# Moving LayerNorm scaling from VectorE to GpSimd and the value eviction to ScalarE in a fused attention and mixture-of-experts block

## The reference

```python
# x: (4, 512, 256), 16 heads of 16, 8 experts, top 1, all float32
h = layernorm(x) * (1 + ca) + sa                 # ca, sa, ... : rows of silu(c) @ wmod, one set per batch
qkv = h @ Wqkv.T + bqkv                          # bqkv: 768 values, the last 256 belong to v
attn = softmax(mask(q k^T / 4)); o = attn v      # causal
x = x + ga * (o @ Wout.T + bout)
h = layernorm(x) * (1 + cb) + sb
x = x + gb * (shared_mlp(h) + s * expert(h))     # expert = argmax of h @ router, s = sigmoid of its logit
```

## Time and profile before

| what | value |
|---|---|
| median of 3 runs | 481.53 us |
| the profiled execution's own time | 479.8 us |
| its span | 478.1 us |
| mean granted TensorE clock | 0.967 of full speed |
| TensorE (PE) busy | 402.4 us, 84% |
| VectorE (DVE) busy | 310.0 us, 65% |
| ScalarE (ACT) busy | 226.8 us, 47% |
| GpSimd (POOL) busy | 209.0 us, 44% |
| chain that ended last | PE 51%, DVE 17%, DMA 8%, POOL 7%, issue 7%, ACT 6% |

### The profile page before, as it was taken

How to read it: one execution, slowest core, us unless ns; L and a number is a source line. 1 busy time by engine, 2 the same in 40 slices (tenths; PEclk the granted TensorE clock), 3 DMA queues, 4 the chain that set the end, 5 groups by cost and what they waited for, 6 DMA issues and landing times.

```text
span 478.1 us, 8357 instructions
## 1 busy us (share of the span) xinstructions
PE 402.4 (84%) x2898; PEld 227.9 (48%) x2898; DVE 310.0 (65%) x629; ACT 226.8 (47%) x403; POOL 209.0 (44%) x251
## 2 busy tenths in 40 slices
PE   3767677889978789988879968999968999999991
PEld 3233233444544345444434434565645666666661
DVE  3823697876898968999977753789734444444441
ACT  2533424867666666755677636345122232323220
POOL 1457393374226763358331762110600555555332
PEclk9997789999999999998999989999989999999998
DMA  8568548765678557652433001994621344434210
GB/s 258 170 154 212 147 117 259 265 196 136 168 264 293 156 127 167 222 179 88 169 81 99 2 0 52 354 360 161 180 86 44 65 80 85 78 74 81 32 21 0
DMA packets 45921, 67.95 MB, mean 142 GB/s; under 512 B 5365, under 2 KB 33653, under 8 KB 45881
## 3 DMA queue, kind: packets, MB, share of 16 engines
q1 hardware_dynamic: 40200, 58.76, 40.6%
q0 software_dynamic: 5152, 8.14, 8.6%
q10 hardware_dynamic: 528, 0.52, 0.3%
HBM read 43.14 MB, written 25.18 MB: 143 GB/s over the span
## 4 chain that ended last, share of the span: by engine, by line
PE 51%; DVE 17%; DMA 8%; POOL 7%; issue 7%; ACT 6%; SPq 3%; ACTq 0%; DVEq 0%; POOLq 0%
PE bank L1411 35%; DVE mx L1066 5%; PE bank L1525 4%; PE bank L1509 3%; DVE rowg L1167 2%; PE bank L1739 2%; PE bank L1481 2%; DMA qk_d<-W 2%; POOL W L719 2%; DMA w_d<-rowg 2%; DMA mod_d<-h2T 1%; ACT rowg L896 1%; DMA stage<-in_gup 1%; POOL rowg L727 1%; POOL rowg L726 1%
## 5 line engine op out<-in xcount | busy, mean ns | idle before, releaser
L846 ACT ACTIVATE W<-bank 128x512 f32<-128x512 f32 (+1 forms) x176 | 94.8, 564 | 65.1 <-PE bank L1509 63.3
L1066 DVE TENSOR_REDUCE mx<-bank 128x1 f32<-128x384 f32 (+3 forms) x176 | 104.8, 632 | 20.2 <-PE bank L1483 19.9
L1411 PE MATMUL bank<-W 128*128 128x256 f16 (+2 forms) x756 | 106.5, 293 | 10.2 <-POOL W L694 3.4
L1411 PEld LDWEIGHTS bank<-W 128*128 128x128 f16 x756 | 73.3, 100 | 44.3 <-issue 14.2
L1481 PE MATMUL bank<-W 126*128 126x128 f16 (+3 forms) x256 | 67.0, 318 | 20.6 <-DVE mx L1066 17.2
L719 POOL TENSOR_SCALAR_AFFINE_SELECT W<-W 128x512 f32<-128x512 f32 x64 | 45.3, 713 | 79.7 <-ACT W L846 79.7
L1411 PE MATMUL bank<-W,h2T 128*128 x276 | 68.4, 385 | 4.9 <-DVE W L1182 4.0
L1509 PE MATMUL bank<-W 128*128 128x512 f16 (+3 forms) x256 | 63.1, 304 | 5.2 <-ACT W L846 3.5
L789 POOL DMA_INDIRECT out<-h2T,sidx x23 | 36.3, 1578 | 69.5 <-DVE h2T L1381 69.2
L1525 PE MATMUL bank<-W 128*32 128x128 f32 (+3 forms) x512 | 48.4, 451 | 8.7 <-POOL W L719 8.7
L1483 PE MATMUL bank<-maskb,identb 128*128 128x128 bf16 (+2 forms) x176 | 45.3, 257 | 0.0
(11 more groups left out here) (163 smaller groups left out, 522.7 us busy)
## 6 DMA issues: line engine op xcount, KB each, us to landing
w_d<-rowg SPq DMA_DIRECT2D x18, 512.0 KB, 3.9
W<-w_d SPq DMA_DIRECT2D x18, 512.0 KB, 8.0
stage<-in_gup SPq DMA_DIRECT2D x16, 512.0 KB
qk_d<-W SPq DMA_DIRECT2D x48, 128.0 KB
W<-qk_d SPq DMA_DIRECT2D x32, 192.0 KB, 4.4
stage<-in_down SPq DMA_DIRECT2D x8, 512.0 KB
x_sb<-in_x SPq DMA_DIRECT2D x4, 512.0 KB, 8.9
h_d<-gbb SPq DMA_DIRECT2D x4, 512.0 KB, 4.5
```

The source lines that it names most:

```text
L846: a.activation(PT[j][:, i:i + m, :], t_bank(N)[:, 0:m * w].rearrange("p (i n) -> p i n", i=m), ACT.Exp).then_inc(s_exp, 1)
L1066: v.tensor_reduce(mx_v[:, b % 2, hp0 // 4, par, i:i + m, t], SB[N % 3][:, 0:m * w].rearrange("p (i n) -> p i n", i=m), AX.X, ALU.max).then ...
L1411: i = t_.matmul(outp, l, r, start=(n == 0), stop=(n == len(prods) - 1), **kw)
```

## The change

Both normalisations are computed by GpSimd: `norm1` moves there as it is, and what `scale2` did becomes the first of three instructions of GpSimd's `modulate2`. The eviction of the values moves to ScalarE, one scaled copy of 128x512 in place of two VectorE instructions of 128x256, and no bias is added. The value bias is instead multiplied by the output weights once, by two float32 matmuls of TensorE in the lead (`value_bias`), and VectorE adds the row to the output bias. The broadcast load of the value bias is gone (`bvb`), and its semaphore count falls from 48 to 32. The signature, the new semaphores and the list of inputs change to suit and are left out here.

```diff
@@ -162,7 +162,7 @@
         cs = sb("cs", [P, 2, KC, B])
         sac = sb("sac", [P, KC, B])
         cac = sb("cac", [P, KC, B])
-        bqk = sb("bqk", [P, 4])
+        bqk = sb("bqk", [P, 6])
         st1 = sb("st1", [P, NT, 6])
         mv1 = sb("mv1", [P, NT, 2])
         ve1 = sb("ve1", [P, NT])
@@ -221,7 +221,7 @@
         h1 = early(2 * KC * S, F16).rearrange("p (s k n) -> p s k n", s=2, k=KC)
         h32 = early(KC * S).rearrange("p (k n) -> p k n", k=KC)
         q32 = h32
-        bvb = early(H)
+        at[0] += 2 * H
         qk16 = early(4 * 2 * S, F16).rearrange("p (a c n) -> p a c n", a=4, c=2)
 
         qs, ks, v1 = [], [], []
@@ -442,7 +444,6 @@
             sp.dma_start(wm[:, :, 0:2 * H], wmod_v[:, :, 0:2 * H]).then_inc(s_wm, 16)
             sp.dma_start(wq_s, wqkvT.rearrange("(k p) n -> p k n", p=P)).then_inc(s_wq, 16)
             sp.dma_start(bqk[:, :], bqkc).then_inc(s_bias, 16)
-            sp.dma_start(bvb, bqkv[2 * H:3 * H].partition_broadcast(P)).then_inc(s_bias, 16)
             sp.dma_start(boutb, bout.partition_broadcast(P)).then_inc(s_bias, 16)
             sp.dma_start(wm[:, :, 2 * H:6 * H], wmod_v[:, :, 2 * H:6 * H]).then_inc(s_wmr, 16)
             sp.dma_start(wo_s, woutT.rearrange("(k p) n -> p k n", p=P)).then_inc(s_wo, 16)
@@ -667,6 +668,16 @@
                 link(g.tensor_scalar(ve[:, c], mv[:, c, 1], EPS, 0.0, ALU.add, ALU.add))
                 g.tensor_tensor(rs[:, c], ve[:, c], neghalf[:, :], ALU.pow).then_inc(done, 1)
 
+            def norm1(b):
+
+                po.wait_ge(s_rstd, b + 1)
+                if b:
+                    po.wait_ge(s_xt, KC * b)
+                for t in range(TT):
+                    n = TT * b + t
+                    g.tensor_scalar(xn[:, t], x_sb[:, n], mv1[:, n, 0:1], rs1[:, n:n + 1],
+                                    ALU.subtract, ALU.mult).then_inc(s_xn, 1)
+
             def modulation_rows(part):
 
                 if part == 0:
@@ -705,7 +716,7 @@
                 po.wait_ge(s_bc[b % 2], 16 * (b // 2 + 1))
                 po.wait_ge(s_xn, TT * (b + 1))
                 if b == 0:
-                    po.wait_ge(s_bias, 48)
+                    po.wait_ge(s_bo, 1)
                 link(g.tensor_tensor(bga, boutb, bc[:, b % 2, 0:H], ALU.mult))
                 for t in range(TT):
                     i = g.tensor_tensor(x_sb[:, TT * b + t], x_sb[:, TT * b + t], bga, ALU.add)
@@ -722,7 +733,11 @@
             def modulate2(b, t):
 
 
-                po.wait_ge(s_hm, TT * b + t + 1)
+                n = TT * b + t
+                if t == 0:
+                    po.wait_ge(s_rstd2, b + 1)
+                link(g.tensor_scalar(h2f[:, t], x_sb[:, n], mv2[:, n, 0:1], rs2[:, n:n + 1],
+                                     ALU.subtract, ALU.mult))
                 link(g.tensor_tensor(h2f[:, t], h2f[:, t], bc[:, b % 2, 2 * H:3 * H], ALU.mult))
                 g.tensor_tensor(h2f[:, t], h2f[:, t], bc[:, b % 2, H:2 * H], ALU.add).then_inc(s_h2, 1)
 
@@ -735,6 +750,7 @@
                 g.tensor_scalar(h2s[:, t], h2f[:, t], srow[:, n:n + 1], 0.0, ALU.mult, ALU.add).then_inc(s_rows, 1)
 
             rstd(ve1, mv1, rs1, 0, s_mv, s_rstd)
+            norm1(0)
             h_low(0, 0)
             h_low(0, 1)
             for u in range(4):
@@ -751,6 +767,8 @@
                     for job, c, k in side_jobs(b, n):
                         if job == "stats1":
                             rstd(ve1, mv1, rs1, c, s_mv, s_rstd)
+                        elif job == "norm1":
+                            norm1(c)
                         elif job == "turn":
                             h_low(c, k)
                         elif job == "qk":
@@ -835,6 +853,16 @@
                     a.activation(dst, side_bank("qk", b, u)[:, :], ACT.Identity,
                                  bias=bqk[:, 2 * isk + u // 2:2 * isk + u // 2 + 1],
                                  scale=1.0 / WS if isk else 0.25 / WS).then_inc(s, 1)
+
+            def v_out(b, k):
+                ac.wait_ge(s_qkv, 6 * b + 5 + k)
+                if k == 0 and b < 2:
+                    ac.wait_ge(s_const, 3 + b)
+                if k == 0 and b >= 2:
+                    ac.wait_ge(s_pv, 16 * (b - 1))
+                dst = v1[b % 2][:, NH * 17 * 2 * k:NH * 17 * 2 * (k + 1)].rearrange("p (t h d) -> p t h d", t=2, d=17)
+                a.activation(dst[:, :, :, 0:HD], M1[:, :].rearrange("p (t h d) -> p t h d", t=2, d=HD), ACT.Copy,
+                             scale=1.0 / WS).then_inc(s_v, 2)
 
             def exps(N):
                 G, n = N // UNITS, N % UNITS
@@ -928,7 +956,9 @@
                     if n % UNITS == 4 and G > 0:
                         outs(G - 1)
                     for job, c, k in side_jobs(b, n):
-                        if job == "turn":
+                        if job == "v":
+                            v_out(c, k)
+                        elif job == "turn":
                             h_parts(c, k)
                         elif job == "qk":
                             qk_parts(c, k)
@@ -1011,33 +1041,10 @@
                     i = v.bn_aggr(mv1[:, TT * b + t], st1[:, TT * b + t])
                 i.then_inc(s_mv, 1)
 
-            def norm1(b):
-                ve.wait_ge(s_rstd, b + 1)
-                ve.wait_ge(s_mv, b + 1)
-                if b:
-                    ve.wait_ge(s_xt, KC * b)
-                for t in range(TT):
-                    n = TT * b + t
-                    v.tensor_scalar(xn[:, t], x_sb[:, n], mv1[:, n, 0:1], rs1[:, n:n + 1],
-                                    ALU.subtract, ALU.mult).then_inc(s_xn, 1)
-
-            def v_out(b, k):
-                ve.wait_ge(s_qkv, 6 * b + 5 + k)
-                if k == 0 and b < 2:
-                    ve.wait_ge(s_const, 3 + b)
-                if k == 0 and b >= 2:
-                    ve.wait_ge(s_pv, 16 * (b - 1))
-                for t in (2 * k, 2 * k + 1):
-                    dst = v1[b % 2][:, NH * 17 * t:NH * 17 * (t + 1)].rearrange("p (h d) -> p h d", d=17)
-                    src = M1[:, H * (t % 2):H * (t % 2 + 1)].rearrange("p (h d) -> p h d", d=HD)
-                    v.scalar_tensor_tensor(dst[:, :, 0:HD], src, 1.0 / WS,
-                                           bvb.rearrange("p (h d) -> p h d", d=HD),
-                                           ALU.mult, ALU.add).then_inc(s_v, 1)
-
             def modulation_columns():
 
                 ve.wait_ge(s_mc, 1)
-                ve.wait_ge(s_bias, 48)
+                ve.wait_ge(s_bias, 32)
                 v.tensor_copy(sac[:, :, :], T2[:, 0:8].rearrange("p (k b) -> p k b", k=KC))
                 v.tensor_scalar(cac[:, :, :], T2[:, 8:16].rearrange("p (k b) -> p k b", k=KC),
                                 1.0, None, ALU.add)
@@ -1049,6 +1056,9 @@
                                        ALU.subtract).then_inc(s_wl, 1)
 
             def low_others():
+                ve.wait_ge(s_bv, 1)
+                ve.wait_ge(s_bias, 32)
+                v.tensor_tensor(boutb, boutb, OTb[:, 0:H], ALU.add).then_inc(s_bo, 1)
                 ve.wait_ge(s_wh, 3)
                 v.scalar_tensor_tensor(wo16[:, 1], wo_s, WS, wo16[:, 0], ALU.mult, ALU.subtract)
                 v.scalar_tensor_tensor(rw16[:, 1], rw_s[:, :, :], WS, rw16[:, 0], ALU.mult,
@@ -1119,13 +1129,6 @@
                     i = v.bn_aggr(mv2[:, TT * b + t], st2[:, TT * b + t])
                 i.then_inc(s_mv2, 1)
 
-            def scale2(b, t):
-                n = TT * b + t
-                ve.wait_ge(s_mv2, b + 1)
-                ve.wait_ge(s_rstd2, b + 1)
-                v.tensor_scalar(h2f[:, t], x_sb[:, n], mv2[:, n, 0:1], rs2[:, n:n + 1],
-                                ALU.subtract, ALU.mult).then_inc(s_hm, 1)
-
             def centre2(b):
 
                 ve.wait_ge(s_mv2, b + 1)
@@ -1135,7 +1138,7 @@
                                            ALU.subtract, ALU.mult).then_inc(s_hm, 1)
 
             def modulate2(b):
-                ve.wait_ge(s_hm, TT * (b + 1))
+                ve.wait_ge(s_hm, TT)
                 ve.wait_ge(s_rstd2, b + 1)
                 for t in range(TT):
                     n = TT * b + t
@@ -1217,7 +1220,6 @@
                     add_shared(TT * b + t)
 
             stats1(0)
-            norm1(0)
             modulation_columns()
             low_qkv()
 
@@ -1236,20 +1238,14 @@
                     for job, c, k in side_jobs(b, n):
                         if job == "max":
                             negate(c, k)
-                        elif job == "v":
-                            v_out(c, k)
                         elif job == "stats1":
                             stats1(c)
-                        elif job == "norm1":
-                            norm1(c)
                         elif job == "attn":
                             attn_low(c, k)
                         elif job == "out":
                             residual(c, k)
                         elif job == "stats2":
```

(15 more changed lines are left out.)

10 lines of the change are left out of this document (6 added, 4 removed).

## The result

The changed kernel takes 497.04 us in the median of 4 runs, against 481.18 us for the kernel before beside it (4 runs): a ratio of 1.032 [1.028, 1.036], 15.9 us slower. The forecast was 483.6 us with 476.8 to 488.0 as its range, and even the slow-form rival stopped at 490.9. The profiled execution took 496.05 us with a span of 494.3, against 478.1 before.

The account below looks back on a forecast made before the run. TensorE and VectorE were near full, but the order of instructions, above all masks queued on GpSimd, was taken to decide. The sum -0.3 - 0.8 + 3.2 = +2.1 us on 481.53 gave 483.6 us, range 476.8 to 488.0.

Parts of the forecast that it names:

- slow-form rival: GpSimd's moved scalings take 1.08 us each, as a tensor-scalar with constants does: 490.9 us, chance 0.10.
- The step that failed: Pricing GpSimd's new scaling at 0.48 us, from an existing tensor-scalar of the same 128x256 shape.
- the first norms: First normalisations on GpSimd, in the lead and batches 0 and 1: covered, cost 0; uncovered 0.5 in the lead.
- the clock: TensorE's longer idling can bring one more stretch at the lower clock: at most 1.6 us, in the range only.
- GpSimd's new work: Ten second scalings of 0.56 us ahead of late masks in batches 1 to 3, less 2.4: +3.2 us, bounds 0 and 5.6.
- 2.4 us of pauses: GpSimd's waits for VectorE's second scaling, 2.4 us over all, go away and are subtracted from its added work.
- `value_bias`: Two float32 matmuls in the lead, covered by TensorE's 2.84 us wait for the stacked heads: 0, uncovered +0.9 us.
- Values and first stall: Batch 1, TensorE's 1.73 us stall before 133.89: ScalarE's copy delays its split, so the gain is 0.3 us, not 1.7.
- Second stall: Batch 1, TensorE's 1.38 us stall before 140.15: VectorE's split starts 1.1 us sooner without the scalings; gain 0.8 us.
- VectorE is what counts: Rival: TensorE's three stalls of batch 1 come back whole, 3.4 us, giving 478.1 us; chance 0.26.
- Collisions: Rival: the 28 new GpSimd instructions meet about 4 VectorE splits on shared ports, +2.0 us, giving 485.6; chance 0.13.

Follow-up runs that it names:

- e1: The kernel before with twelve forms of GpSimd's tensor-scalar appended at its end, three times each, nothing beside them: subtract-mult 1.22 us, mult-add 0.40 to 0.55.
- e2: The changed kernel with the first normalisation back on VectorE: 489.57 us, 1.017 of the kernel before.
- e4: The changed kernel with both normalisations back on VectorE, leaving the value copy on ScalarE and the bias through the output projection: 480.15 us, 0.996 of the kernel before.
- e3: The changed kernel with the second scaling back on VectorE: 483.77 us, 1.005 of the kernel before.

## Why the prediction was wrong

**The step that failed** is one sentence: "I take 0.48, since it has the new instruction's own 128x256 shape." It chose between two rows by their tile. By e1 the number of rows hardly matters and the operation pair does, so L679, add-add with constants, was the nearer row of the two, and even it was 0.14 short, twice the 0.07 of a per-partition operand. The price is 1.22 us alone, 1.30 and 1.37 in place. Two terms that the sum had at nothing failed with it: the first norms and the clock.

The terms of the sum, each with what it measured:

- *GpSimd's new work, forecast +3.2.* The masks that TensorE waited for came 9.1 us later (4.16, 3.87 and 1.03). The place (masks behind `modulate2`) and the count (4, 4 and 2) were right. With the price corrected, 10 x (1.30 + 0.08) less the 2.4 us of pauses, the model gives 11.4, so it is still 2.3 high, half of it in batch 3. One cause can be read there: the second `modulate2`'s first product took 1.64 us and the mask 1.08 before (276.05 and 278.58), 0.72 and 0.64 after. The gauges read: the wait 1.35 became 2.68 (forecast 2.6), but it is one of three where there was one, and the sum is 16.3 where I gave 12.
- *The clock, kept out of the sum and at 1.6 us at most in the range.* Behind the masks it made the other 3.8 us of the steps, as the rows after the table show. That 10 x 1.30 = 13.0 lies so near to the 12.8 us of the steps is therefore chance: it counts neither the pauses nor the clock. No run isolates the clock, but the same work without a wait took 3.66 us at 0.50 and 1.97 at 1.00.
- *The first norms, forecast 0.* They cost 3.1 us in the lead, where the cover was 3.3 us wide (7.83 to 11.11) and the four now take 6.24. The norm of batch 1, also in the lead, was priced nowhere: its four take 4.83 us from 32.84, TensorE's turn waits 2.98 us for them at 37.82, and the wait of 2.84 for the stacked heads, which was to cover `value_bias`, is used up. The first `scores` come at 38.70, where I gave 35.2. The turns of batches 2 and 3 wait 2.45 and 0.74. In all it is 4.9 us by the traces and 7.7 by the medians. The four at 7.89 are longer than 4 x 1.22 = 4.9 as the last of them took 2.62, with VectorE's two-input L1055 (11.29 to 13.04) beside it:

```profile
7.89 6.24 POOL L678 TENSOR_SCALAR W<-x_sb,mv,rs 128x256 f32<-128x256 f32 x4
...
14.18 1.97 PE L1439 MATMUL bank<-ident,W 128*128 128x128 f32 x8 [3.16 <-POOL W L678]
```

- *Values and first stall, forecast -0.3.* VectorE's split started at 134.45 after the change, that is 130.8 with the 3.7 us of shift taken off, against 131.30 before; the stall went from 1.73 to 1.53. Nearly as forecast, and not the 1.7 us at first sight. The order on ScalarE is as read: copy at 132.88, split at 133.37.
- *Second stall, forecast -0.8.* It went from 1.38 to 1.26. Both stalls and the work between them brought TensorE 0.56 us forward (140.15 before, 143.21 after, 3.06 apart where `turn_out` had been 3.62), of 1.1 forecast, and at once the turn of 145.51 waits 0.74 us for GpSimd's first norm: the next `turn_out` is 3.66 late again, and nothing is left. The relieved VectorE waits for ScalarE's split, and that waits for a transfer, which I had seen for batch 0 and not asked for here:

```profile
139.63 1.06 ACT L924 ACTIVATE rowg<-stage 128x1024 f16<-128x1024 f32 x1 [0.83 <-DMA w_d<-rowg]
```

```profile
140.72 1.23 DVE L1170 SCALAR_TENSOR_TENSOR rowg<-stage,rowg 128x1024 f16<-128x1024 f32 x1 [1.09 <-ACT rowg L924]
```

- *`value_bias`, forecast 0 of at most 0.9.* With `norm1` back on VectorE the four `turn_out` of batch 0 are 0 to 0.4 us early in e2 and 0.1 to 0.5 late in e4, so it is covered within that scatter.

**The rivals.** The slow form was the right one, with a chance of 0.10 and at 490.9 (its +1.3 for the lead is 1.4 by its own figures): with its own price corrected to 1.30 + 0.08 it gives 481.53 - 1.1 + 10 x 1.38 - 2.4 for the masks, plus 3.1 for the lead, 494.9. That this is so near to 497.0 is again partly luck, since the masks have 2.3 us too much in it and the clock nothing. Its chance was too low since the argument against it was one row (L735) whose operations were not compared with the new instruction's. "VectorE is what counts" has no support: in the table above the difference never falls by more than 0.6 us from one row to the next, and the values alone (e4) won 1.7 us in all. "Collisions" as a loss spread over all instructions is out by e3 and by the price of 1.22 us alone in e1, though e2's time lay near it. That single instructions are held up is seen (1.22 becomes 1.30 and 1.37), worth 16 x 0.15 + 12 x 0.08 = 3.4 us of GpSimd time, of which the ten scalings of the steps carry about 0.8.

The Trainium skill, GPSIMD Engine Reference, section 4.1 Engine selection, sets elementwise work on GpSimd beside VectorE and says of it that "1-input is roughly line-rate". For mult-add the runs come near to that (0.40 us with constants and 0.55 with two per-partition operands, beside 0.41 for VectorE's subtract-mult); for subtract-mult they don't, 1.22 against 0.41, and the measurement decides.

## What to carry to other kernels

Price a moved instruction by a row with the same operations on the same engine, not by one with the same tile; where no such row exists, the far bound deserves a real chance. If a normalisation must be on GpSimd, negate the mean once and use add-mult. Then look at what stands behind it in that queue: work put ahead of something that the bound engine waits for delayed it by most of its length here (9.1 of 13.8 us), the wait cost TensorE's clock on top (3.8 us), and moving it later in the queue is worth trying before moving it to another engine (here 0.7% for three numbers in a table).
